# Last attention product in three split products, its layer norm tile by tile, and the order of the work around it

## What is computed

```python
x = x + _L0_gnn_ref(_layernorm(x), ...)      # softmax aggregation, two-layer MLP
x = x + _L0_ffn_ref(_layernorm(x), ...)      # experts
x = x + _L1_gnn_ref(_layernorm(x), ...)      # graph convolution
x = x + _L1_ffn_ref(_layernorm(x), ...)      # experts
x = x + _L2_gnn_ref(_layernorm(x), ...)      # graph attention: 8 heads, then 1 head
x = x + _L2_ffn_ref(_layernorm(x), ...)      # soft mixture over 32 slots, on rows of unit length
x = x + _L3_gnn_ref(_layernorm(x), ...)      # relational graph convolution, 3 times
x = x + _L3_ffn_ref(_layernorm(x), ...)      # experts
```

```python
h = (x @ W.T).reshape(n, heads, out_ch)
e = leaky_relu(a_src[src] + a_dst[dst], 0.2)
ex = exp(e - segment_max(e, dst)[dst])
alpha = ex / (segment_sum(ex, dst)[dst] + EPS)
out = segment_sum(alpha[:, :, None] * h[src], dst) + bias
...
Xn = X / (sqrt(sum(X * X)) + 1e-6)           # slot layer, X the layer norm of x
```

## Time and profile before

| | |
|---|---|
| profiled execution | 1924.63 us (span 1922.5) |
| median of 3 runs | 1925.05 us |
| TensorE busy | 1804.2 us, 94% of the span |
| VectorE, ScalarE, GpSimd busy | 904.1, 460.1, 689.8 us |
| chain that ended last | TensorE 74%, VectorE 12%, ScalarE 3% |
| mean granted TensorE clock | 0.959 |
| HBM read, written | 96.08 MB, 1.92 MB |

### The profile page before, as it was taken

How to read it: one execution, slowest core, us unless ns; L and a number is a source line. 1 busy time by engine, 2 the same in 40 slices (tenths; PEclk the granted TensorE clock), 3 DMA queues, 4 the chain that set the end, 5 groups by cost and what they waited for, 6 DMA issues and landing times.

```text
span 1922.5 us, 26920 instructions
## 1 busy us (share of the span) xinstructions
PE 1804.2 (94%) x10741; PEld 1657.1 (86%) x10741; DVE 904.1 (47%) x1919; ACT 460.1 (24%) x874; POOL 689.8 (36%) x425
## 2 busy tenths in 40 slices
PE   6799999999989997798899999999999999998999
PEld 6699988998988987685857789999999999997899
DVE  8982234327653679735447691212422242225431
ACT  3533122212132247712203321100111111112220
POOL 1028644553344531032000052353533353344454
PEclk9899999999999998899689998999999999999999
DMA  2002211323111210006000011121211111111112
GB/s 81 1 26 67 76 58 58 125 66 134 52 49 55 66 42 25 1 17 156 1 10 1 1 49 39 48 68 43 65 43 42 58 58 50 50 50 51 58 58 74
DMA packets 41728, 99.60 MB, mean 52 GB/s; under 512 B 10354, under 2 KB 11991, under 8 KB 41618
## 3 DMA queue, kind: packets, MB, share of 16 engines
q1 hardware_dynamic: 37828, 87.87, 15.1%
q10 hardware_dynamic: 3790, 10.14, 1.5%
HBM read 96.08 MB, written 1.92 MB: 51 GB/s over the span
## 4 chain that ended last, share of the span: by engine, by line
PE 74%; DVE 12%; ACT 3%; PEld 2%; issue 2%; POOL 1%; PEldq 0%; DVEq 0%; ACTq 0%; POOLq 0%
PE bank L2103 9%; PE bank L2104 9%; PE bank L2105 9%; PE banks L2103 8%; PE banks L2104 7%; PE banks L2105 7%; PE banks L2201 6%; PE bank L2201 5%; PE bank L2624 3%; PE banks L2624 3%; DVE edge_scores L1718 2%; PE banks L2539 1%; PEld bank L2335 1%; PEld banks L2335 1%; PE bank L2583 1%
## 5 line engine op out<-in xcount | busy, mean ns | idle before, releaser
L734 POOL TENSOR_TENSOR w_hi<-raw,ones_r 128x768 fp32r<-128x768 f32 (+1 forms) x192 | 295.2, 1537 | 1173.6 <-PE banks L2105 620.9
L737 POOL TENSOR_TENSOR w_lo<-raw,w_hi 128x768 fp32r<-128x768 f32 (+1 forms) x192 | 372.6, 1940 | 15.1
L2103 PE MATMUL bank<-w_hi,xT_hi 128*125 128x384 f32 (+2 forms) x614 | 207.2, 337 | 3.9 <-DVE acc L2040 1.6
L2104 PE MATMUL bank<-w_lo,xT_hi 128*125 128x384 f32 (+2 forms) x614 | 206.0, 335 | 0.0
L2105 PE MATMUL bank<-w_hi,xT_lo 128*125 128x384 f32 (+2 forms) x614 | 205.8, 335 | 0.0
L2103 PE MATMUL banks<-w_hi,xT_hi 128*125 128x384 f32 (+2 forms) x426 | 148.0, 347 | 1.6 <-issue 0.8
L2104 PE MATMUL banks<-w_lo,xT_hi 128*125 128x384 f32 (+2 forms) x426 | 147.3, 346 | 0.0
L2105 PE MATMUL banks<-w_hi,xT_lo 128*125 128x384 f32 (+2 forms) x426 | 147.2, 346 | 0.0
L2103 PEld LDWEIGHTS bank<-w_hi,xT_hi 128*125 128x125 f32 x614 | 114.5, 187 | 9.9 <-issue 2.3
L2104 PEld LDWEIGHTS bank<-w_lo,xT_hi 128*125 128x125 f32 x614 | 114.5, 187 | 2.6
L2105 PEld LDWEIGHTS bank<-w_hi,xT_lo 128*125 128x125 f32 x614 | 114.5, 186 | 2.5
(11 more groups left out here) (517 smaller groups left out, 3989.7 us busy)
## 6 DMA issues: line engine op xcount, KB each, us to landing
raw<-wa SPq DMA_DIRECT2D x92, 384.0 KB, 3.0
raw<-wc SPq DMA_DIRECT2D x76, 384.0 KB, 3.0
raw<-wb SPq DMA_DIRECT2D x28, 448.0 KB, 3.3
w_rows<-w_in ACTq DMA_DIRECT2D x1, 3072.0 KB, 12.7
bias<-bias_in ACTq DMA_DIRECT2D x6, 384.0 KB
w_first<-w_in ACTq DMA_DIRECT2D x1, 2304.0 KB, 8.8
w_down<-w_down_in SPq DMA_DIRECT2D x8, 288.0 KB, 5.2
w_up<-w_up_in SPq DMA_DIRECT2D x1, 2304.0 KB, 16.5
```

The source lines that it names most:

```text
L734: pool.tensor_tensor(w_hi[:, k, 0:width], raw[:, k, 0:width], ones[:, 0:1].to_broadcast([P, width]), ALU.mult).then_inc(S("unit_high"), 1)
L737: pool.tensor_tensor(w_lo[:, k, 0:width], raw[:, k, 0:width], f(w_hi[:, k, 0:width]), ALU.subtract).then_inc(S("unit_split"), 1)
L2103: pe.matmul(dst, l_hi, r_hi, start=start, stop=False)
L2104: pe.matmul(dst, l_hi, r_lo, start=False, stop=False)
```

## The change

- The last attention product runs as three split products. ScalarE rounds the last weights and the second projection's rows (`last_hi`, `h2_hi`), VectorE takes the rests (`last_lo`, `h2_lo`).
- The slot layer's norm is taken tile by tile as the second half of each tile is added, with the unit length folded in one factor, r = 1 / (sqrt(D v) + 1e-6 sqrt(v + eps)). ScalarE writes the rows.
- The masks of a head are two operations, over 2 and 3 source tiles (`PARTS`), instead of five.
- The scores of heads 6 and 7 both stand beside head 0, and the shift parts of heads 4 to 7 ahead of head 1; two source broadcasts move one group up.
- Head 7 is turned inside the second projection, behind its step (0, 0). The score rows, sources and shifts move up in it; the score columns are turned ahead of the source broadcast. In VectorE's list the bias and the slot parameters' scaling now stand ahead of them, in ScalarE's the slots' root.
- GpSimd splits the second projection's units only when the last mask of head 7 is done.

The diff, cut to its core:

```diff
-SOURCES_AT = {3: (0, 1), 5: (2,), 7: (3,), 8: (4,), 10: (5,), 12: (6,), 14: (7,)}
+SOURCES_AT = {3: (0, 1), 5: (2,), 7: (3,), 8: (4,), 10: (5,), 11: (6,), 13: (7,)}
...
-LAST_ROWS, LAST_SOURCES, LAST_SHIFTS, LAST_SHIFT = (0, 4), (0, 6), (1, 1), (1, 3)
+LAST_TURN, LAST_ROWS, LAST_SOURCES, LAST_SHIFTS, LAST_SHIFT = (0, 0), (0, 2), (0, 4), (1, 0), (1, 1)
+PARTS = ((0, 2), (2, NT))
...
-        if h:
+        if 0 < h < HEADS:
...
+            several_from("g2p_outT", 2 * (HEADS - 1), 2, "g2p_relu")
             for i in range(2):
                 add("g2q_rows", i, "g2q_rows_low", i + 1)
+            pairs("g2q_colT")
...
+        h2_hi = at_("h2_hi", [TN, NT, 2 + D], f32r, NM)
+        h2_lo = [at_(f"h2_lo{c}", [TN, NT, 386 - 2 * c], f32r, NM + 15424 + c * 7744) for c in range(2)]
...
+        last_lo = at_("last_lo", [TN, NT, NP], f32r, XT)
+        last_hi = at_("last_hi", [TN, NT, NP], f32r, XT + up32(NT * NP * 4))
...
-            ring_units(pool, after, UNITS_A - after, split(UNIT, n_shared))
+            second = FIRST_UNIT["d", "g2b"]
+            for u in range(after, second):
+                split(UNIT, n_shared)(u, u // RING, u % RING)
+            pool.wait_ge(*E("g2p_prob", len(PARTS) * HEADS))
+            ring_units(pool, second, UNITS_A - second, split(UNIT, n_shared))
...
                 if h < HEADS:
                     shifts("g2p", h)
+                    if h == 2:
+                        shift_rows("g2p", 1)
                     for s in range(NT):
                         powers("g2p", h, s)
-                    if h == 2:
-                        shift_rows("g2p", 1)
                 if h >= 3:
                     head_out(h - 3)
...
+            act.wait_ge(*E("slots_squared", 1))
+            act.activation(slot_sum, slot_sum, ACT.Sqrt).then_inc(S("slots_norm"), 1)
+            act.wait_ge(*E("g2_bias_used", 1))
+            act.dma_start(bias8[0:8, :], rows_in[24:32, :]).then_inc(S("f2_bias_full"), 16)
...
+                    act.activation(h2_hi[:, n, 2 + c * 384:2 + (c + 1) * 384], bank("g2b", c * NT + n)[0:TN, 0:384],
+                                   ACT.Copy).then_inc(S("g2_h2_high"), 1)
...
-            for s in range(NT):
-                powers("g2q", 0, s)
+            for s in range(NT + 2):
+                if s < NT:
+                    powers("g2q", 0, s)
+                if s >= 2:
+                    act.wait_ge(*E("last_full", s - 1))
+                    act.activation(last_hi[:, s - 2], prob[0][:, s - 2], ACT.Copy).then_inc(S("last_high"), 1)
             second_rows(1)
 
-            act.wait_ge(*E("slots_squared", 1))
-            act.activation(slot_sum, slot_sum, ACT.Sqrt).then_inc(S("slots_norm"), 1)
-            act.wait_ge(*E("g2_bias_used", 1))
-            act.dma_start(bias8[0:8, :], rows_in[24:32, :]).then_inc(S("f2_bias_full"), 16)
-            root_of_variance("f2")
-            for n in range(NT):
-                act.wait_ge(*E("f2_xn", n + 1))
-                if n:
-                    act.wait_ge(*E("f2_squared", n))
-                act.activation(f2_junk[:], xn[:, n], ACT.Square, accum_out=sum8[0:TN, n:n + 1]
-                               ).then_inc(S("f2_squared"), 1)
-            act.wait_ge(*E("f2_squared", NT))
-            act.activation(sum8[0:TN], sum8[0:TN], ACT.Sqrt).then_inc(S("f2_norm"), 1)
-            xT_high("f2_xT", KD)
+            def unit_rows(n):
+                variance = moments[0:TN, 2 * n + 1:2 * n + 2]
+                act.wait_ge(*E("f2_aggregated", n + 1))
+                act.activation(spread[0:TN, n:n + 1], variance, ACT.Sqrt, scale=float(D))
+                act.activation(rstd[0:TN, n:n + 1], variance, ACT.Sqrt, bias=ln_eps[0:TN]).then_inc(S("f2_std"), 1)
+                act.wait_ge(*E("f2_centre", n + 1))
+                act.activation(xn[:, n], x[0:TN, n], ACT.Identity, bias=centre[0:TN, n:n + 1],
+                               scale=rstd[0:TN, n:n + 1]).then_inc(S("f2_xn"), 1)
+
+            for n in range(NT - 1):
+                unit_rows(n)
+            tile_high("f2_xT", KD, 0)
+            unit_rows(NT - 1)
+            for n in range(1, NT):
+                tile_high("f2_xT", KD, n)
...
+            def greater_branch(layer, h, s):
+
+                pr, made = prob_of(layer, h), NT * h + s
+                dve.wait_ge(*E(layer + "_powers", made + 1))
+                STT(pr[:, s], pr[:, s], 3.0, lesser[:, made % 3], ALU.min, ALU.max).then_inc(S(layer + "_greater"), 1)
+
+            def weights_of_edges(h, beside=()):
+
+                pr = prob_of("g2p", h)
+                for s in range(NT):
+                    greater_branch("g2p", h, s)
+                    for a, b in PARTS:
+                        if s == b - 1:
+                            dve.wait_ge(*E("g2p_greater", NT * h + b))
+                            STT(pr[:, a:b], pr[:, a:b], 3.0, f(adj[:, a:b]), ALU.min, ALU.mult
+                                ).then_inc(S("g2p_prob"), 1)
+                    for other, d in beside[2 * s:2 * s + 2]:
+                        if d == 0:
+                            await_group(dve, "g2p_asB", 2 * other + 1)
+                        greatest_score("g2p", other, d)
+
+            def weights_of_last():
+
+                pr = prob[0]
+                for s in range(NT + 2):
                     if s < NT:
-                        dve.wait_ge(*E(layer + "_powers", made + 1))
-                        STT(pr[:, s], pr[:, s], 3.0, lesser[:, made % 3], ALU.min, ALU.max
-                            ).then_inc(S(layer + "_greater"), 1)
-                    if s:
-                        dve.wait_ge(*E(layer + "_greater", made))
+                        greater_branch("g2q", 0, s)
+                    if 1 <= s <= NT:
+                        dve.wait_ge(*E("g2q_greater", s))
                         STT(pr[:, s - 1], pr[:, s - 1], 3.0, f(adj[:, s - 1]), ALU.min, ALU.mult
-                            ).then_inc(S(layer + "_prob"), 1)
-                    if beside is not None and s < NT:
-                        greatest_score(layer, beside, s)
+                            ).then_inc(S("last_full"), 1)
+                    if s >= 2:
+                        dve.wait_ge(*E("last_high", s - 1))
+                        TT(last_lo[:, s - 2], pr[:, s - 2], f(last_hi[:, s - 2]), ALU.subtract
+                           ).then_inc(S("g2q_prob"), 1)
 
             rows_low("g2p")
...
-            for h in range(2):
-                weights_of_edges("g2p", h, beside=HEADS - 2 + h)
+            weights_of_edges(0, [(h, d) for h in range(HEADS - 2, HEADS) for d in range(NT)])
             shift_parts("g2p", 1, HEADS)
+            weights_of_edges(1)
...
-            rows_low("g2q")
-            greatest_scores("g2q", 0)
-            score_columns("g2q")
-            shift_parts("g2q", 0, 1)
             dve.wait_ge(*E("g2_xn", NT))
             dve.wait_ge(*E("g2_bias_full", 16))
             add_bias("g2")
-            await_group(dve, "g2p_agg", 2 * HEADS - 1)
-            dve.memset(h2[:, :, 0:2], 1.0).then_inc(S("h2_ones"), 1)
-            weights_of_edges("g2q", 0)
+            await_group(dve, "g2p_outT", 2 * HEADS - 1)
...
+            rows_low("g2q")
+            score_columns("g2q")
+            greatest_scores("g2q", 0)
+            shift_parts("g2q", 0, 1)
+
+            def second_low(c):
+                if c == 0:
+                    dve.memset(f(h2_hi[:, :, 0:2]), 1.0).then_inc(S("h2_ones"), 1)
+                    dve.memset(f(h2_lo[0][:, :, 0:2]), 0.0).then_inc(S("h2_ones"), 1)
+                else:
+                    dve.wait_ge(*E("g2q_uvB_read", 4))
+                for n in range(NT):
+                    dve.wait_ge(*E("g2_h2_high", c * NT + n + 1))
+                    TT(h2_lo[c][:, n, 2 - 2 * c:386 - 2 * c], bank("g2b", c * NT + n)[0:TN, 0:384],
+                       f(h2_hi[:, n, 2 + c * 384:2 + (c + 1) * 384]), ALU.subtract).then_inc(S("g2_h2"), 1)
+
+            second_low(0)
+            weights_of_last()
+            second_low(1)
...
-                if c:
-                    dve.wait_ge(*E("g2_x", i + 1))
+                dve.wait_ge(*E("g2_x", i + 1))
+                if c == 0:
                     node_stats(n, 0)
-                    last = node_stats(n, 1)
-            link(last)
-
+                    continue
+                measure("f2", n)
+                dve.wait_ge(*E("f2_aggregated", n + 1))
+                dve.wait_ge(*E("f2_std", n + 1))
+                r = rstd[0:TN, n:n + 1]
+                link(STT(r, r, 1e-6, spread[0:TN, n:n + 1], ALU.mult, ALU.add))
+                link(dve.reciprocal(r, r))
+                STT(centre[0:TN, n:n + 1], moments[0:TN, 2 * n:2 * n + 1], -1.0, r, ALU.mult, ALU.mult
+                    ).then_inc(S("f2_centre"), 1)
 
             clear_pad("f2_xT_pad")
-            layer_norm("f2", lambda n: xn[:, n], True)
-            dve.wait_ge(*E("f2_xn", NT))
-            dve.wait_ge(*E("f2_norm", 1))
```

(32 more changed lines are left out.)

31 lines of the change are left out of this document (10 added, 21 removed).

## The result

The changed kernel takes **1907.47 us** (median of 4, 1897.59 to 1910.05) against 1925.35 of the kernel before: ratio 0.9899 with a 95% interval of 0.9863 to 0.9936, 17.9 us faster. Forecast were 29.6 us and 1895.4. The median lies 0.5 us above the upper end of the range, 1907; the ratio, taken of the 1925.05 us that the forecast started from, gives 1905.6, inside it. The direction and most parts were right; 12 us of the gain are missing, and they had to be found.

A forecast was written before the change was run, and what follows sets the result against it. TensorE's matmul stream, busy 94% of the span, was taken as the bound. Gains 10.3 + 5.7 - 2 + 6.1 + 9.5 = 29.6 us, from a median of 1925.05, gave 1895.4 us; range 1887 to 1907.

The forecast's parts named there:

- Parts 1 to 3: Head phase: late unit splits, new order of first heads, merged masks; ScalarE starts head 4's copies 5.9 us earlier, masks lose 0.5.
- part 1: GpSimd's unit splits wait for head 7's last mask, taking 3 x 2.2 = 6.5 us off VectorE in the head phase.
- part 2: New order of first heads: the 9.53 us hole at the shift columns goes, but group 11's shift broadcast comes 2.4 us later.
- Merged masks: Two mask operations a head instead of five on VectorE: no gain, 0.5 us lost once before head 7's product.
- Part 4: Last head turned inside the second projection: start at 803.8, 10.3 us earlier; length 52.6 us against 58.3.
- New waits in it: Second projection: VectorE's bias and slot scaling ahead of score rows' low halves, late splits, shift columns; 2 us charged, bounds 0 and 6.
- the rival of the failed cover: Split weights or low rows come 4 to 8 us after TensorE is ready, plus 2.6 us of low clock: 1904 us; chance 0.20.
- Part 5: Last product as 150 split matmuls: 26.5 us, 6.1 us gained, with split weights covered by 1 us.
- Part 6: Layer norm tile by tile, from the last product's end to the logits: 13.1 us against 22.6, 9.5 us gained, bounds 7 and 11.
- Their time passes through unchanged: Ahead of 705 us and behind 928 us, instructions of the same kind and number remain, so their time stays as before.
- The heads give nothing: Head phase: ScalarE has no idle time and the start may be pushed back, so 5.9 us becomes 0: 1901.3 us; chance 0.13.
- The slower case: Second projection to last product: more than 207 of 390 matmuls at 1.2 GHz would eat the 29.6 us; chance 0.03.

The follow-up runs named there:

- the repeat: The changed kernel run again with nothing edited: 1906.29 us, ratio 0.9896 to the kernel before.
- without part 1: The changed kernel, but GpSimd splits the second projection's first units without waiting for head 7's last mask: 1909.58 us, ratio 0.9913 to the kernel before.
- without part 2: The changed kernel with the old order of the first heads' scores, shift columns and source broadcasts: 1902.52 us, ratio 0.9874 to the kernel before.

## Why the prediction was off

In the profiled executions, the terms of the sum against the stretches (forecast, measured, in us of gain; the measured sum is of unrounded times):

| | forecast | measured |
|---|---|---|
| ahead of the first row | 0 | -1.2 |
| first row to second projection | 10.3 | 10.8 |
| second projection with its new waits | 3.7 | 1.2 |
| last product | 6.1 | 6.1 |
| tail | 9.5 | 2.3 |
| behind the logits | 0 | -4.7 |
| sum | 29.6 | 14.4 |

**Parts 1 to 3, heads.** The sum was right, the reasons only in part. The hole closed and ScalarE became the engine that is late: it begins the copies of head 4 at 62.0 us behind the first row against 68.7 before, 6.7 earlier where 5.9 were forecast, and has no wait above 0.3 us from 745 to 795. But the walk laid the gain on both parts together, while without part 1 it is 3.5 us less and without part 2 nothing less: of the 6.5 us taken off VectorE 3.5 arrive, and part 2 gives less than it costs, with a wait at group 11 forecast at 2.4 and measured at 1.90. Merged masks: 0.5 us forecast, 1.0 measured, absorbed later.

**Part 4.** Start forecast at 803.8, came at 804.60. The length without new waits was forecast as 52.6 us; the kernel with the slots moved has 52.1. The term "New waits in it" was mis-sized: charged with 2 us, it was 5.0, inside its bounds of 0 and 6. The place was named (slots' scaling ahead of the low rows, cover under 1 us), and it was walked with 4 us for the slots. They took 6.5 (818.96 to 825.50): the split beside them stretched eight scalings to 3.77 us, which take 0.84 in the kernel before, and the bias ahead of them took 6.07 instead of 5. Nor did the walk have a low clock behind the wait. This is the rival of the failed cover, at one of its places and below its price of 6 and 2.6.

**Part 5.** 26.5 us as said, with 0.7 us of cover where 1 was forecast. Three passes in place of the four of *FP8 and Floating Point Precision* of the Trainium skill (TensorE Precision Notes) would have given 24.5; the row decided rightly.

**Part 6.** This is where the largest part of the gain was missed: 7.2 of the 15.2 us by which the profiled gain is short. The term that was mis-sized is the splits beside the tail's chain. With the wide splits the tail took 17.3 and 20.4 us in the changed kernel, where 13.1 were taken and the bounds were 11.6 and 15.6. The blocks were foreseen ("two or three such blocks"), as 1.15 us each, from an earlier norm. They were two of 1.4 and 2.0 us in one profile and four in the other, and they are paid more than once: the chain that starts late meets the next split too, and behind TensorE's waits its clock is low. Undisturbed the tail takes 11.9 to 14.6 us. The 11.6 forecast for it are near the low end by luck in part: the terms named for it (2.75, 0.9, four copies of 0.95, 2.6) add up to 10.1, and 1.5 of it have no source.

**Behind the logits.** "Their time passes through unchanged" is the step that was wrong in kind. The same instructions took 4.7 us longer in this profile and 3.7 in the repeat; over all profiles with the same instructions it is from 2.0 less to 7.1 more. Of the 4.7, 3.5 lie between the logits and the first degree count (226.9 us against 223.4), where in 40 to 45 us behind the logits' copy the granted clock is 0.50 against 0.77 before. A range for this kernel needs room for that, and mine had none. Why the clock comes back at different times is open.

**Rivals.** The failed cover happened in part. "The heads give nothing" did not. The slower case, a clock that stays low in the projection, did not: it was 0.69 for 5.5 us there, which is under the 0.8 that was named as a sign of being wrong.

## What to carry to other kernels

When a change brings the bound engine forward, walk every queue that feeds it at its new time, background work of GpSimd included: an operation of 0.16 us with two SBUF inputs lasts as long as the split that it meets, and a chain of such operations meets the next one too. Background work with time to spare (the wide splits are wanted over 100 us later) should wait for an event behind the critical chain; here one wait gave back 5.4 us, or 2.5 where fewer blocks were met, and one reordered block 5.0. A part can look worthless when undone alone, or useful, because another wait absorbs the difference: compare stretches between fixed rows, and undo it again once that wait is gone.
